# Second attention of a two-layer network: steps that cover one key tile of both heads of a pair

## The chip, the cores and the metric

The kernel runs on one core of one Trainium2 chip. The metric is the device time of one execution in microseconds, median over runs. TensorE is called PE here, VectorE DVE, ScalarE ACT and GpSimd POOL, as in the profile.

## The reference

Six stages follow each other on x of shape (8, 512, 128): expert feed-forward, banded attention, expert feed-forward, then a second kind of feed-forward, a second attention and that feed-forward again. Only the second attention is touched. It has 16 heads of 8 dimensions, for each of 8 chunks of 512 rows:

```python
q_norm_sq = jnp.sum(q * q, axis=-1, keepdims=True)
k_norm_sq = jnp.sum(k * k, axis=-1)[:, :, None, :]
qk = jnp.einsum('bhnd,bhmd->bhnm', q, k)
diff_sq = jnp.maximum(q_norm_sq + k_norm_sq - 2.0 * qk, 0.0)
denom = jnp.maximum((1.0 - CURV * q_norm_sq) * (1.0 - CURV * k_norm_sq), 1e-06)
cosh_arg = jnp.maximum(1.0 + 2.0 * CURV * diff_sq / denom, 1.0)
distance = jnp.where(cosh_arg > 1.0, jnp.arccosh(jnp.maximum(cosh_arg, 1.0 + 1e-12)), 0.0)
attn = jax.nn.softmax(-distance, axis=-1)
out = jnp.einsum('bhnm,bhmd->bhnd', attn, v)
```

With u = diff_sq / denom, the weight is (sqrt(u) + sqrt(1 + u)) to the power -2, which the kernel computes as a root, a root, a sum, a logarithm and an exponential.

## The kernel before

The second attention is the function `attn1`. A chunk has 16 heads, and for each head a matrix of 512 keys (4 key tiles of 128 partitions) by 512 queries. It is worked off in four bursts (b0 to b3) of four heads. A burst has 8 steps; a step covers two key tiles (a half) of one head, so head h = n // 2 and half = n % 2 for step n. The engines run these programs, each in its own order, joined by semaphores:

- PE, `difference(n)` (line 1605): two matmuls with 28 rows of K into two PSUM banks, banks 0 and 1 or 2 and 3 in turn. They read partitions r to r + 28 of KT and QT, where r = 64 * (h % 2). `factor(n)` (line 1617): two matmuls with 9 rows from partition r = 64 * (h % 2) + 32 into banks 4 and 5. The start partition is what sets the row group of the array, so both matmuls of a step use the same one.
- DVE, `relu(n)` (line 1477): U = max(difference, 0), from PSUM into one of four U slots, 1024 elements a partition. `scale(n)` (line 1485): U = min(factor, clamp) * U. The order is relu(n0), then for i = 0 to 7: relu(n0 + i + 1), scale(n0 + i), and then the work that `after0` to `after3` hang on step i: copies of turned rows (line 1321), the OUT copy (line 1383), the division, the norm's copy.
- ACT: for the first two heads of a burst Y = sqrt(U + 1) (line 1443) and U = sqrt(U) (line 1444) head by head, then the same for the last two heads in one (the joined root, 4096 elements a partition), a table load, then the logarithm (line 1449) and the exponential (line 1451) for each pair, and a table load back.
- POOL: Y = Y + U for each head (line 1401), which frees the head's U slot (`t_ready`); between bursts it prepares rows.
- PE, `outputs` (line 1587): the products of weights and values of a pair of heads, for the key tiles named, into bank 7 (OUT). At the end of a pair they free its two Y slots (`pvh_done`). There are six Y slots; the joined root of a burst waits for the products of the pair of three pairs earlier. Even pairs stand inside a burst (`pair_in_burst`), odd ones in the window between bursts, before the first factor of the next burst.
- The window between bursts on PE: `ahead` (two differences of the next burst), then for b0 and b3 `turn_four` (four blocks of transposes, line 1313, copied by DVE), for b1 the projections (line 1206), on whose results DVE works before its first relu, for b2 the output projection (line 458), whose sum and statistics DVE takes before its first relu; then a pair's products.

Inside bursts PE also has transposes hung on single steps: turns at i = 0 to 3 of b0 and b3, the division's in b1 and its turn back at i = 4, the norm's turn (i = 4) and scores (line 1376, i = 5) in b3.

Of the kernel before, what the change touches and what calls it, by code (L numbers as in the profile page):

```python
# [5 lines left out]
ALU = mybir.AluOpType  # L6
# [7 lines left out]
P = 128  # L14
B, S, D = 8, 512, 128
TOK = B * S
TPC = S // P
TILES = TOK // P
H, HD = 16, 8
# [15 lines left out]
def macaron(nc, x, alpha, w_qkv0, bias_rows0, wo0, wo0_t, wfc0, router0, expert_bias, up0, down0,  # L35
            w_qkv1, wo1, router1, up1, down1, out, stop_after=99):
    ctx = ExitStack()
    with ctx:
# [6 lines left out]
        ps = ctx.enter_context(nc.psum_tensor("ps", [P, 8, 512], F32))  # L45
# [1083 lines left out]
        def attn1():  # L1129
            name, lay, nxt = "A1", 1, 1  # L1130
            s = sems[name]
# [3 lines left out]
            UR, YR = 4, 6  # L1135
            SETS = H // 4
            PAIRS = H // 2
            ROWS = 6
            HALVES = 2 * H
            TURNS = 2 * GR  # L1140
            EARLY = TURNS // 2
            VC = 16
            with ExitStack() as st:
# [7 lines left out]
                QT = ab("QT", [P, GR, S], F32R)  # L1151
                KT = ab("KT", [P, GR, S], F32R)
                OT = ab("OT", [P, SETS, S])
                Um = ab("U", [P, UR, TPC, S])
# [37 lines left out]
                    return ps[:, bank, :].rearrange("p (h d) -> p h d", d=HD)  # L1192

                def d_pair(n):
                    return ps[:, 2 * (n % 2):2 * (n % 2) + 2, :].rearrange("p b q -> p (b q)")

                def g_pair():
                    return ps[:, 4:6, :].rearrange("p b q -> p (b q)")

                def u_half(h, half):  # L1200
                    return Um[:, h % UR, 2 * half:2 * half + 2, :].rearrange("p t q -> p (t q)")


                def project_rows_tensor(eng, src, part, bank, done):
# [180 lines left out]
                def body(block):  # L1385
# [46 lines left out]
                    @block.scalar  # L1432
                    def _(eng):
                        def main(c, m, first):
                            for h0 in range(0, H, 4):
                                for h in (h0, h0 + 1, h0 + 2):
                                    joined = h == h0 + 2
                                    y = y_two(m, h) if joined else flat(y_slot(m, h))
                                    u = u_two(h) if joined else flat(Um[:, h % UR])
                                    if not first or h >= YR:  # L1440
                                        eng.wait_ge(s["pvh_done"], c * PAIRS + h // 2 - 1)
                                    eng.wait_ge(s["u_ready"], c * HALVES + 2 * h + (4 if joined else 2))
                                    eng.activation(y, u, ACT.Sqrt, bias=1.0)  # L1443
                                    eng.activation(u, u, ACT.Sqrt).then_inc(s["s_ready"], 2 if joined else 1)  # L1444
                                eng.preload_act_table_set("natural_log_exp_and_others")
                                for h in (h0, h0 + 2):
                                    y = y_two(m, h)
                                    eng.wait_ge(s["t_ready"], c * H + h + 2 + UR)
                                    eng.activation(y, y, ACT.Ln)
                                    eng.drain()  # L1450
                                    eng.activation(y, y, ACT.Exp, scale=-2.0).then_inc(s["y_exp"], 2)  # L1451

                        main(0, 0, True)
                        main(1, 1, False)
                        with eng.Fori(0, (B - 2) // TURN) as k:
                            for i in range(TURN):
                                main(TURN * k + (i + 2), (i + 2) % TURN, False)
                        barrier(eng, b0)

                    @block.vector  # L1460
                    def _(eng):
# [6 lines left out]
                        def main(c, m, first):  # L1468
# [1 line left out]
                            before_c = last_chunk(c)  # L1470

                            def relu(n):
                                h, half = n // 2, n % 2
                                if half == 0:
                                    eng.wait_ge(s["t_ready"], c * H + h + 1)
                                eng.wait_ge(s["d_done"], c * HALVES + n + 1)
                                eng.tensor_scalar(u_half(h, half), d_pair(n), 0.0, None,  # L1477
                                                  ALU.max).then_inc(s["dp_vector"], 1)

                            def scale(n):  # L1480
                                h, half = n // 2, n % 2
                                eng.wait_ge(s["g_done"], c * HALVES + n + 1)
                                eng.wait_ge(s["dp_vector"], c * HALVES + n + 1)
                                u = u_half(h, half)
                                eng.scalar_tensor_tensor(out=u, in0=g_pair(), scalar=CLAMP, in1=u, op0=ALU.min,  # L1485
                                                         op1=ALU.mult).then_inc(s["u_ready"], 1)

# [13 lines left out]
                            def after0(i):  # L1501
                                if i < 4:
                                    turned_vector(eng, c, EARLY + 4 + i)
                                if tail and i == 4:
                                    out_copy_vector(eng, c - 1, 2)
                            burst(0, after0)

# [17 lines left out]
                                add_back_vector(eng, c, before_c)  # L1525

                            def after2(i):
                                if i == 4:
                                    out_copy_vector(eng, c, 0)
                            burst(2, after2)  # L1530

# [4 lines left out]
                            def after3(i):  # L1536
                                if i < 4:
                                    turned_vector(eng, c + 1, 4 + i)
                                if i == 4:
                                    out_copy_vector(eng, c, 1)  # L1540
                                    if tail:
                                        copy_norm_vector(eng, c)
                                if tail and i == 5:
                                    norm_logits_vector(eng, s, c, before_c, nxt, ROWS)
                            burst(3, after3)
# [22 lines left out]
                    def _(eng):  # L1568
# [23 lines left out]
                        def main(c, m, first):  # L1592
                            before_m = (m + TURN - 1) % TURN

                            def difference(n):

                                h, half = n // 2, n % 2
                                if half == 0 and h % 2 == 0:
                                    eng.wait_ge(s["turned"], c * TURNS + h + 2)
                                if not (first and n < 2):  # L1600
                                    eng.wait_ge(s["dp_vector"], c * HALVES + n - 1)
                                r = 64 * (h % 2)
                                for b in range(2):
                                    kt = 2 * half + b
                                    last = eng.matmul(ps[:, 2 * (n % 2) + b, :], KT[r:r + 28, h // 2, kt * P:(kt + 1) * P],  # L1605
                                                      QT[r:r + 28, h // 2, :], start=True, stop=True)
                                last.then_inc(s["d_done"], 1)

                            def factor(n):

                                h, half = n // 2, n % 2
                                if not (first and n == 0):
                                    eng.wait_ge(s["u_ready"], c * HALVES + n)
                                r = 64 * (h % 2) + 32
                                for b in range(2):
                                    kt = 2 * half + b
                                    last = eng.matmul(ps[:, 4 + b, :], KT[r:r + 9, h // 2, kt * P:(kt + 1) * P],  # L1617
                                                      QT[r:r + 9, h // 2, :], start=True, stop=True)
                                last.then_inc(s["g_done"], 1)

                            def burst(g, after):
# [20 lines left out]
                                turn_tensor(eng, k, i0 + 3, WINDOW_BANKS[3])  # L1642

                            def pair_in_burst(n, m, pair, i):
                                if i in (5, 6):
                                    outputs(n, m, pair, (i - 5,))
                                if i == 7:
                                    outputs(n, m, pair, (2, 3))


# [1 line left out]
                            eng.wait_ge(s["turned"], c * TURNS + EARLY)  # L1652
                            if not first:
                                eng.wait_ge(s["lg_copied"], c + 1)
                                eng.wait_ge(s["u_ready"], c * HALVES)
# [17 lines left out]
                            eng.wait_ge(s["u_ready"], c * HALVES + 8)  # L1673
# [31 lines left out]
                            eng.wait_ge(s["u_ready"], c * HALVES + 24)  # L1705
# [111 lines left out]
```

## Time and profile before

| | us |
|---|---|
| median of 3 runs | 3403.89 |
| lowest, highest | 3403.35, 3407.71 |
| profiled execution, its own time | 3406.81 |
| its span in the trace | 3405.1 |
| PE busy | 2960.9 |
| DVE busy | 2218.9 |
| ACT busy | 1886.1 |
| POOL busy | 875.4 |

Busy times are sums over the whole program, of which the second attention is about a third (from 1828 us to some 2960 us). They don't say which engine bounds a stage; waits and timelines do. PE's busy time is made of modelled latencies, so a high share isn't a sign of a full array.

### The profile page before, as it was taken

What the parts mean: (1) busy time and instruction counts of PE and PEld (TensorE: products, weight loads), DVE (VectorE), ACT (ScalarE), POOL (GpSimd) and SP (SyncE); (2) the same over time, 40 slices, a digit from 0 to 9 for tenths busy, and PEclk for the clock granted to TensorE, in tenths of its full rate; (3) what the DMA queues carried; (4) which work ended last, traced back from release to release, by engine and by line L of the source; (5) the groups of instructions that cost most, each with busy time, mean ns of one, the idle gap of its engine ahead of it and who ended that gap; (6) DMA issues with size and microseconds to landing.
All of it is one profiled execution on the core that took longest, in us unless ns stands there. A gap on an engine that the chain in (4) does not pass through costs nothing. (4 is left out here: it accounts for less than half of the span.)

```text
span 3405.1 us, 52318 instructions
## 1 busy us (share of the span) xinstructions
PE 2960.9 (87%) x17860; PEld 2181.0 (64%) x17862; DVE 2218.9 (65%) x5046; ACT 1886.1 (55%) x2052; POOL 875.4 (26%) x584
## 2 busy tenths in 40 slices
PE   5999968888769998799995889898898888489999
PEld 4888846666668887699993333333343333279998
DVE  5555557777645555666666677777777777366665
ACT  2222246767622222343343989989898898533333
POOL 1000010000000000200003566666665667310000
PEclk9999979999979999899996666666666666599999
DMA  2000000000000000000000000000000000100000
GB/s 81 0 0 0 0 1 1 0 0 0 0 0 0 0 0 11 39 0 0 0 0 0 1 0 1 1 0 1 0 1 0 0 0 0 50 1 0 0 0 25
DMA packets 3224, 18.43 MB, mean 5 GB/s; under 512 B 1088, under 2 KB 2112, under 8 KB 2112
## 3 DMA queue, kind: packets, MB, share of 16 engines
q1 hardware_dynamic: 3136, 17.32, 1.3%
q8 instruction: 48, 0.79, 0.1%
q14 instruction: 40, 0.33, 0.0%
HBM read 15.22 MB, written 2.10 MB: 5 GB/s over the span
## 5 line engine op out<-in xcount | busy, mean ns | idle before, releaser
L1401 POOL TENSOR_TENSOR A_Y<-A_Y,A_U 128x2048 f32<-128x2048 f32 x86 | 389.5, 4551 | 260.3 <-ACT A_U L1444 260.3
L1617 PE MATMUL ps<-A_QT,A_KT 9*128 9x512 f32 x512 | 287.1, 655 | 141.8 <-DVE A_U L1485 108.8
L140 POOL TENSOR_TENSOR rstd<-var_eps,half_neg 128x4 f32<-128x4 f32 x45 | 49.8, 1107 | 1208.6 <-DVE var_eps L120 1183.0
L1485 DVE SCALAR_TENSOR_TENSOR A_U<-ps,A_U 128x1024 f32<-128x1024 f32 x256 | 311.4, 1217 | 69.4 <-PE ps L1617 69.4
L1477 DVE TENSOR_SCALAR A_U<-ps 128x1024 f32<-128x1024 f32 x256 | 308.8, 1217 | 59.3 <-PE ps L1605 58.3
L1617 PEld LDWEIGHTS ps<-A_QT,A_KT 9*128 9x128 f32 x512 | 117.1, 283 | 293.2 <-DVE A_U L1485 234.0
L257 ACT ACTIVATE F1b_act<-ps 128x512 f32<-128x512 f32 x256 | 153.3, 599 | 248.0 <-PE ps L223 232.0
L257 ACT ACTIVATE F1a_act<-ps 128x512 f32<-128x512 f32 x256 | 153.2, 599 | 242.8 <-PE ps L223 226.5
L1605 PE MATMUL ps<-A_QT,A_KT 28*128 28x512 f32 x512 | 262.2, 622 | 1.8 <-DVE A_KT L1321 1.6
L257 ACT ACTIVATE F0b_act<-ps 128x512 f32<-128x512 f32 x160 | 95.7, 598 | 272.8 <-PE ps L223 272.8
L257 ACT ACTIVATE F0a_act<-ps 128x512 f32<-128x512 f32 x160 | 95.7, 598 | 265.1 <-PE ps L223 265.1
L231 PEld LDWEIGHTS ps<-dn,F1a_hT 128*128 128x128 f32 x2048 | 237.2, 192 | 4.4
L231 PEld LDWEIGHTS ps<-dn,F1b_hT 128*128 128x128 f32 x2048 | 237.2, 192 | 4.4
L1587 PE MATMUL ps<-A_Y,A_VA 128*32 128x512 f32 x688 | 238.3, 839 | 1.9 <-ACT A_Y L1451 1.9
L231 PE MATMUL ps<-dn,F1a_hT 128*128 128x128 f32 x2048 | 237.6, 275 | 0.0
L231 PE MATMUL ps<-dn,F1b_hT 128*128 128x128 f32 x2048 | 237.6, 275 | 0.0
L1444 ACT ACTIVATE A_U<-A_U 128x2048 f32<-128x2048 f32 (+1 forms) x96 | 236.5, 2463 | 0.0
L1401 POOL TENSOR_TENSOR dn<-dn,A_U 128x2048 f32<-128x2048 f32 x42 | 190.5, 4560 | 134.0 <-ACT A_U L1444 134.0
L841 ACT ACTIVATE A_M<-A_M,A_nmax 128x192 f32<-128x192 f32 (+1 forms) x512 | 203.8, 471 | 34.8 <-DVE A_nmax L956 33.4
L1443 ACT ACTIVATE A_Y<-A_U 128x2048 f32<-128x2048 f32 (+1 forms) x64 | 159.4, 2490 | 83.0 <-DVE A_U L1485 45.1
L1605 PEld LDWEIGHTS ps<-A_QT,A_KT 28*128 28x128 f32 x512 | 116.3, 274 | 137.9 <-issue 120.1
L956 DVE CUSTOM_DVE_ANT_0 A_M<-ps,A_mask 128x192 f32<-128x192 f32 (+1 forms) x512 | 169.3, 387 | 50.1 <-PE ps L1007 49.3
(336 smaller groups left out, 6704.1 us busy)
## 6 DMA issues: line engine op xcount, KB each, us to landing
dn<-in_down SPq DMA_DIRECT2D x2, 2048.0 KB, 12.5
stage<-in_up SPq DMA_DIRECT2D x1, 2560.0 KB, 9.4
X<-in_x SPq DMA_DIRECT2D x1, 2048.0 KB, 7.7
F1a_up<-in_up SPq DMA_DIRECT2D x1, 2048.0 KB, 8.0
F1b_up<-in_up SPq DMA_DIRECT2D x1, 2048.0 KB, 8.0
out_x<-X SPq DMA_DIRECT2D x1, 2048.0 KB, 6.3
dn<-in_down SPq DMA_DIRECT2D x1, 1280.0 KB, 12.0
qkv_w_s<-in_w_qkv SPq DMA_DIRECT2D x2, 192.0 KB
```

The lines of the kernel that those rows point to most:

```text
L231: last = eng.matmul(ps[:, 4 + d % 2, t * P:(t + 1) * P], hT[:, d % 2, hb, t * P:(t + 1) * P], dn[:, d, hb, :], start=(hb == 0), stop=(hb = ...
L257: eng.activation(act_out[:, j % RING, :], ps[:, (j * G) % 4, :], ACT.Silu if lay == 0 else ACT.Relu).then_inc(s["act_done"], 1)
L841: last = eng.activation(m, m, ACT.Exp, scale=-1.0, bias=nmax[:, n % MR, b, r:r + 1])
L956: last = eng.tensor_tensor_reduce(M[:, n % MR, b, r, w0:w1], ps[:, 2 * (n % 2) + b, r * WIN + w0:r * WIN + w1], mask[:, w0:w1], -1.0, 3e38 ...
L1401: eng.tensor_tensor(flat(y_slot(m, h)), flat(y_slot(m, h)), flat(Um[:, h % UR]), ALU.add).then_inc(s["t_ready"], 1)
L1443: eng.activation(y, u, ACT.Sqrt, bias=1.0)
L1444: eng.activation(u, u, ACT.Sqrt).then_inc(s["s_ready"], 2 if joined else 1)
L1477: eng.tensor_scalar(u_half(h, half), d_pair(n), 0.0, None, ALU.max).then_inc(s["dp_vector"], 1)
L1485: eng.scalar_tensor_tensor(out=u, in0=g_pair(), scalar=CLAMP, in1=u, op0=ALU.min, op1=ALU.mult).then_inc(s["u_ready"], 1)
L1587: last = eng.matmul(ps[j:j + 32, OUT, :], VA[:, v0:v0 + 32], y_slot(m, h)[:, kt, :], start=(kt == 0), stop=(kt == TPC - 1))
L1605: last = eng.matmul(ps[:, 2 * (n % 2) + b, :], KT[r:r + 28, h // 2, kt * P:(kt + 1) * P], QT[r:r + 28, h // 2, :], start=True, stop=True)
L1617: last = eng.matmul(ps[:, 4 + b, :], KT[r:r + 9, h // 2, kt * P:(kt + 1) * P], QT[r:r + 9, h // 2, :], start=True, stop=True)
```

## The change

A step covers one key tile of both heads of a pair instead of two key tiles of one head. For step n, pair = n // 4 and the key tile kt = n % 4. The two matmuls of a step now read from partitions 0 and 64 (differences) or 32 and 96 (factors). DVE writes key tile kt of two U slots. Waits follow: DVE's first step of a pair waits until the U slots of both heads are free, ACT's roots wait until the four steps of the pair are scaled. `HALVES` becomes `STEPS`, with the same value. The products of the pair inside a burst move from steps i = 5, 6, 7 to 4, 5, 6 (the first key tile after factor 4, the second after factor 5, the last two after factor 6 and so before factor 7). The OUT copies on DVE move from i = 4 to i = 3.

```diff
-                def u_half(h, half):
-                    return Um[:, h % UR, 2 * half:2 * half + 2, :].rearrange("p t q -> p (t q)")
+                def u_step(n):
+                    h, kt = 2 * (n // TPC), n % TPC
+                    return Um[:, h % UR:h % UR + 2, kt, :]
...
-                                    eng.wait_ge(s["u_ready"], c * HALVES + 2 * h + (4 if joined else 2))
+                                    eng.wait_ge(s["u_ready"], c * STEPS + TPC * (h // 2 + 1))
...
                             def relu(n):
-                                h, half = n // 2, n % 2
-                                if half == 0:
-                                    eng.wait_ge(s["t_ready"], c * H + h + 1)
-                                eng.wait_ge(s["d_done"], c * HALVES + n + 1)
-                                eng.tensor_scalar(u_half(h, half), d_pair(n), 0.0, None,
-                                                  ALU.max).then_inc(s["dp_vector"], 1)
+                                pair, kt = n // TPC, n % TPC
+                                if kt == 0:
+                                    eng.wait_ge(s["t_ready"], c * H + 2 * pair + 2)
+                                eng.wait_ge(s["d_done"], c * STEPS + n + 1)
+                                eng.tensor_scalar(u_step(n), d_pair(n), 0.0, None, ALU.max).then_inc(s["dp_vector"], 1)
...
-                                if tail and i == 4:
+                                if tail and i == 3:
                                     out_copy_vector(eng, c - 1, 2)
...
-                                if i == 4:
+                                if i == 3:
                                     out_copy_vector(eng, c, 0)
...
-                                if i == 4:
+                                if i == 3:
                                     out_copy_vector(eng, c, 1)
-                                    if tail:
-                                        copy_norm_vector(eng, c)
+                                if tail and i == 4:
+                                    copy_norm_vector(eng, c)
...
-                                r = 64 * (h % 2)
                                 for b in range(2):
-                                    kt = 2 * half + b
-                                    last = eng.matmul(ps[:, 2 * (n % 2) + b, :], KT[r:r + 28, h // 2, kt * P:(kt + 1) * P],
-                                                      QT[r:r + 28, h // 2, :], start=True, stop=True)
+                                    r = 64 * b
+                                    last = eng.matmul(ps[:, 2 * (n % 2) + b, :], KT[r:r + 28, pair, kt * P:(kt + 1) * P],
+                                                      QT[r:r + 28, pair, :], start=True, stop=True)
...
-                                r = 64 * (h % 2) + 32
                                 for b in range(2):
-                                    kt = 2 * half + b
-                                    last = eng.matmul(ps[:, 4 + b, :], KT[r:r + 9, h // 2, kt * P:(kt + 1) * P],
-                                                      QT[r:r + 9, h // 2, :], start=True, stop=True)
+                                    r = 64 * b + 32
+                                    last = eng.matmul(ps[:, 4 + b, :], KT[r:r + 9, pair, kt * P:(kt + 1) * P],
+                                                      QT[r:r + 9, pair, :], start=True, stop=True)
...
                             def pair_in_burst(n, m, pair, i):
-                                if i in (5, 6):
-                                    outputs(n, m, pair, (i - 5,))
-                                if i == 7:
+                                if i in (4, 5):
+                                    outputs(n, m, pair, (i - 4,))
+                                if i == 6:
                                     outputs(n, m, pair, (2, 3))
```

## Rows read from the trace of the kernel before

**Rows 1.** The page's 40 slices of the span, TensorE's granted clock in tenths.

```profile
PEclk9999979999979999899996666666666666599999
```

**Rows 2.** Waits from 1828 to 2950 us: us in total, times, longest.

```profile
ACT A_Y L1443 <- PE ps L1587: 37.6, 9, 7.4
...
ACT dn L1443 <- PE ps L1587: 23.4, 4, 7.9
```

**Rows 3.** Timeline of ACT: start us, us, instruction, idle before and its releaser.

```profile
1890.98 3.62 ACT L1443 ACTIVATE A_Y<-A_U 128x4096 f32<-128x4096 f32 x1 [3.43 <-PE ps L1587]
...
2356.34 1.91 ACT L1443 ACTIVATE A_Y<-A_U 128x2048 f32<-128x2048 f32 x1
...
2388.46 1.91 ACT L1443 ACTIVATE dn<-A_U 128x2048 f32<-128x2048 f32 x1
...
2396.52 3.62 ACT L1443 ACTIVATE A_Y<-A_U 128x4096 f32<-128x4096 f32 x1 [0.75 <-PE ps L1587]
...
2436.68 3.62 ACT L1443 ACTIVATE dn<-A_U 128x4096 f32<-128x4096 f32 x1 [7.93 <-PE ps L1587]
...
2849.16 3.62 ACT L1443 ACTIVATE dn<-A_U 128x4096 f32<-128x4096 f32 x1 [5.72 <-PE ps L1587]
```

**Rows 4.** Timeline of POOL, b0 of chunk 4.

```profile
2392.25 9.07 POOL L1401 TENSOR_TENSOR dn<-dn,A_U 128x2048 f32<-128x2048 f32 x2 [9.30 <-ACT A_U L1444]
2403.73 9.05 POOL L1401 TENSOR_TENSOR A_Y<-A_Y,A_U 128x2048 f32<-128x2048 f32 x2 [2.41 <-ACT A_U L1444]
```

**Rows 5.** Timeline of DVE, b0 of chunk 4 up to the start of b1.

```profile
2373.25 0.68 DVE L1321 CAST A_QT<-ps 128x512 fp32r<-128x512 f32 x1
2373.85 1.21 DVE L1477 TENSOR_SCALAR A_U<-ps 128x1024 f32<-128x1024 f32 x1
2374.98 1.21 DVE L1485 SCALAR_TENSOR_TENSOR A_U<-ps,A_U 128x1024 f32<-128x1024 f32 x1
...
2380.84 1.21 DVE L1485 SCALAR_TENSOR_TENSOR A_U<-ps,A_U 128x1024 f32<-128x1024 f32 x1
...
2392.88 1.23 DVE L1485 SCALAR_TENSOR_TENSOR A_U<-ps,A_U 128x1024 f32<-128x1024 f32 x1 [1.31 <-PE ps L1617]
2400.44 1.22 DVE L1230 CAST up_hi<-ps 128x1024 fp32r<-128x1024 f32 x1 [6.34 <-PE ps L1206]
...
2409.87 2.35 DVE L1477 TENSOR_SCALAR A_U<-ps 128x1024 f32<-128x1024 f32 x2
```

**Rows 6.** Timeline of PE, the tail of b0 and the window before b1.

```profile
2386.11 1.92 PE L1587 MATMUL ps<-A_Y,A_VA 128*32 128x512 f32 x4
2387.96 0.79 PE L1605 MATMUL ps<-A_QT,A_KT 28*128 28x512 f32 x1
2387.97 0.79 PE L1617 MATMUL ps<-A_QT,A_KT 9*128 9x512 f32 x1
...
2391.62 1.22 PE L1617 MATMUL ps<-A_QT,A_KT 9*128 9x512 f32 x2 [0.59 <-DVE A_U L1485]
...
2396.33 2.07 PE L1605 MATMUL ps<-A_QT,A_KT 28*128 28x512 f32 x4
2398.33 3.48 PE L1206 MATMUL ps<-qkv_w_s,A_xa 128*128 128x128 f32 x16
...
2402.63 3.63 PE L1587 MATMUL ps<-A_Y,A_VA 128*32 128x512 f32 x16
```

**Rows 7.** Timeline, PE and DVE: pieces of b3, of the window before b0, of that before b2.

```profile
2350.65 1.88 PE L1376 MATMUL ps<-rw,xT_c 128*128 128x8 f32 x8
...
2364.68 1.11 PE L1313 MATMUL ps<-ident,up_hi 128*128 128x128 f32 x4
...
2368.67 2.34 DVE L1477 TENSOR_SCALAR A_U<-ps 128x1024 f32<-128x1024 f32 x2
...
2438.48 2.08 PE L458 MATMUL ps<-out_w,A_oT 128*128 128x128 f32 x8
...
2443.08 2.35 DVE L1477 TENSOR_SCALAR A_U<-ps 128x1024 f32<-128x1024 f32 x2
```

More of the change, by code:

```diff
@@ L1138, in attn1 @@
             ROWS = 6
-            HALVES = 2 * H
+            STEPS = 2 * H
             TURNS = 2 * GR
@@ L1194, in d_pair @@
                 def d_pair(n):
-                    return ps[:, 2 * (n % 2):2 * (n % 2) + 2, :].rearrange("p b q -> p (b q)")
+                    return ps[:, 2 * (n % 2):2 * (n % 2) + 2, :]
                 def g_pair():
-                    return ps[:, 4:6, :].rearrange("p b q -> p (b q)")
-                def u_half(h, half):
-                    return Um[:, h % UR, 2 * half:2 * half + 2, :].rearrange("p t q -> p (t q)")
+                    return ps[:, 4:6, :]
+                def u_step(n):
+                    h, kt = 2 * (n // TPC), n % TPC
+                    return Um[:, h % UR:h % UR + 2, kt, :]
                 def project_rows_tensor(eng, src, part, bank, done):
@@ L1472, in relu @@
                             def relu(n):
-                                h, half = n // 2, n % 2
-                                if half == 0:
-                                    eng.wait_ge(s["t_ready"], c * H + h + 1)
-                                eng.wait_ge(s["d_done"], c * HALVES + n + 1)
-                                eng.tensor_scalar(u_half(h, half), d_pair(n), 0.0, None,
-                                                  ALU.max).then_inc(s["dp_vector"], 1)
+                                pair, kt = n // TPC, n % TPC
[3 more added lines that the diff above has]
+                                eng.tensor_scalar(u_step(n), d_pair(n), 0.0, None, ALU.max).then_inc(s["dp_vector"], 1)
                             def scale(n):
[L1481 to L1484, printed above, removed]
+                                eng.wait_ge(s["g_done"], c * STEPS + n + 1)
+                                eng.wait_ge(s["dp_vector"], c * STEPS + n + 1)
+                                u = u_step(n)
                                 eng.scalar_tensor_tensor(out=u, in0=g_pair(), scalar=CLAMP, in1=u, op0=ALU.min,
@@ L1595, in difference @@
                             def difference(n):
-                                h, half = n // 2, n % 2
-                                if half == 0 and h % 2 == 0:
-                                    eng.wait_ge(s["turned"], c * TURNS + h + 2)
+                                pair, kt = n // TPC, n % TPC
+                                if kt == 0:
+                                    eng.wait_ge(s["turned"], c * TURNS + 2 * pair + 2)
                                 if not (first and n < 2):
-                                    eng.wait_ge(s["dp_vector"], c * HALVES + n - 1)
@@ L1602, in difference @@
-                                r = 64 * (h % 2)
+                                    eng.wait_ge(s["dp_vector"], c * STEPS + n - 1)
                                 for b in range(2):
-                                    kt = 2 * half + b
-                                    last = eng.matmul(ps[:, 2 * (n % 2) + b, :], KT[r:r + 28, h // 2, kt * P:(kt + 1) * P],
-                                                      QT[r:r + 28, h // 2, :], start=True, stop=True)
+                                    r = 64 * b
@@ L1607, in difference @@
+                                    last = eng.matmul(ps[:, 2 * (n % 2) + b, :], KT[r:r + 28, pair, kt * P:(kt + 1) * P],
+                                                      QT[r:r + 28, pair, :], start=True, stop=True)
                                 last.then_inc(s["d_done"], 1)
                             def factor(n):
-                                h, half = n // 2, n % 2
+                                pair, kt = n // TPC, n % TPC
                                 if not (first and n == 0):
-                                    eng.wait_ge(s["u_ready"], c * HALVES + n)
@@ L1614, in factor @@
-                                r = 64 * (h % 2) + 32
+                                    eng.wait_ge(s["u_ready"], c * STEPS + n)
                                 for b in range(2):
-                                    kt = 2 * half + b
-                                    last = eng.matmul(ps[:, 4 + b, :], KT[r:r + 9, h // 2, kt * P:(kt + 1) * P],
-                                                      QT[r:r + 9, h // 2, :], start=True, stop=True)
+                                    r = 64 * b + 32
@@ L1654, in main @@
                                 eng.wait_ge(s["lg_copied"], c + 1)
-                                eng.wait_ge(s["u_ready"], c * HALVES)
+                                eng.wait_ge(s["u_ready"], c * STEPS)
                             turn_four(c, EARLY)
@@ L1672, in main @@
                             project_rows_tensor(eng, xa, 0, 6, "q_done")
-                            eng.wait_ge(s["u_ready"], c * HALVES + 8)
+                            eng.wait_ge(s["u_ready"], c * STEPS + 8)
                             project_rows_tensor(eng, xa, 1, 4, "k_done")
@@ L1704, in main @@
                                 eng.wait_ge(s["x_added"], c)
-                            eng.wait_ge(s["u_ready"], c * HALVES + 24)
+                            eng.wait_ge(s["u_ready"], c * STEPS + 24)
                             turn_four(c + 1, 0)
```

## Prediction

> **What bounds the kernel now.** I read the slices of the span first: the second attention holds the slices where the granted clock sits at 6 tenths [rows 1]. PE looks 87% busy there, but those are latencies at a low clock, so I went to the waits of that stretch. ScalarE (ACT) is the engine with least slack: a burst of four heads costs it 2388.46 - 2356.34 = 32.12 us without a stall [rows 3], 128.5 us for the four bursts b0 to b3 of a chunk. Yet from the first b1 to the last (7 chunks) the joined root moves from 1890.98 to 2849.16, which is 136.9 us a chunk [rows 3]. Nearly all of the 8.4 us between is ACT waiting for a Y slot, that is for weight-value products: 37.6 + 23.4 = 61.0 us in 13 waits [rows 2]. The largest sits in b1 (7.93 us at 2436.68) [rows 3].
>
> Why are the products late? The chain is VectorE (DVE) and PE in turn. In a burst's tail (b0 of chunk 4) a factor pair is issued at 2391.62 and its scale starts at 2392.88 [rows 5, 6]: 1.26 us, two matmuls one behind the other in the same row group. In front of it stand the products, 1.85 us of PE per key tile. After the last scale (ends 2394.1) PE still has two key tiles of products until 2396.33, then two differences (2.0 us), then the projections at 2398.33; DVE gets its next work at 2400.44 and starts b1 at 2409.87 [rows 5, 6]. So DVE and PE, not ACT, set the pace.
>
> **The change, part by part.** Let S be the end of a burst's eighth scale, E that of its fourth, J the start of ACT's joined root.
>
> *Pairing.* The two matmuls of a step go to row groups 0 and 64 (factors 32 and 96) instead of one. The trace has such pairs: at 2387.96 and 2387.97 a difference and a factor of different groups start 0.01 us apart, 0.79 us each, and 4 matmuls take the time of two [rows 6]. I take a pair of one kind as the same: 0.59 us of PE (before 1.15), and 0.83 us from issue to DVE (before 1.26). Bounds: 1.15 (no overlap) and 0.59. The DVE operations now write two rows of 512 with a gap; the strided conversion of 1024 elements at 2400.44 takes 1.22 us like the others [rows 5], so 0; adds and roots keep their shapes, 0. No instruction, DMA or semaphore is added.
>
> *Tail with outputs at i = 4, 5, 6.* DVE steps are 1.13 us apart, a 512 copy 0.60 [rows 5]. Times from E, clock low, b0: copy and OUT copy to 1.12, relu 5 to 2.25, scale 4 to 3.38. PE: factor 4 at 0.05, first product waits for the OUT copy (1.25) and ends 3.10, difference 6 visible 3.93; relu 6, scale 5 end 6.19; second product 4.2 to 6.05, difference 7 visible 6.88; relu 7, scale 6 end 9.14; factor 6, then the two last products 7.1 to 10.65; factor 7 visible 11.48; S = 12.7. The same for b2 (no turned copy): 12.1. For b1 the turn back (1.05, as one turn at 2364.68) stands before difference 6: 13.1. For b3 the norm's turn (1.05) and the scores (1.81, 2350.65) stand inside too [rows 7]: 15.0. Before, b0 took 12.06 (2380.84 + 1.21 to 2392.88 + 1.23) [rows 5], so its tail to S gets longer by 0.6 us: the two last products now delay factor 7. The others gain length by the same mechanism. But before, ACT had to wait on for products until S + 2.3; now they end 2.0 us ahead of S, and PE is free at S - 1.45 instead of S + 2.3.
>
> *Windows between bursts.* Two differences need 1.2 instead of 2.0 us, so PE is through at S - 0.25. b1: projection to DVE 2.1, DVE's row work 9.43 (2400.44 to 2409.87) [rows 5, 6]: first relu at S + 11.3 (before 15.8). b0, b3: turn_four waits for S (its banks are the factors'), then 4.0 us (2364.68 to 2368.67) [rows 7]: S + 4.0. b2: project_out to relu 4.6 (2438.48 to 2443.08) [rows 7]: S + 4.3. Before, all three began 3.7 us later on PE's side (S + 2.3 against S - 1.45) and had the 2.0 us of differences ahead.
>
> *First half of a burst.* Nine DVE steps and up to three copies: 12.0 us (b1 11.9; b2 10.3), plus about 1 where factor 0 stands behind a whole pair's products.
>
> Unhindered, the chain would be b0 4.0 + 13.0 + 12.7 = 29.7, b1 11.3 + 11.9 + 13.1 = 36.3, b2 4.3 + 11 + 12.1 = 27.4, b3 4.0 + 13.0 + 15.0 = 32.0: 125.4, under ACT's 128.5.
>
> *The new waits.* relu of a pair's first step now waits for the adds of both heads that leave its U slots; ACT's first root waits for four steps instead of two. The second costs nothing: E lies well before ACT's next burst. The first does cost. GpSimd's last add ends at 2403.73 + 9.05 = 2412.8, 16.3 us after J = 2396.52 [rows 3, 4]. Before, relu 6 needed that one; now relu 4 does, so E >= J + 16.3 + 2.3 = J + 18.6 of the burst before. Behind relu 4 on DVE stand the scales, the turned copies and the OUT copy, and PE's second half waits for them. Then S >= J + 18.6 + tail, against the next root at J + 32.12:
> - b0: 31.3, no wait, S 0.8 ahead of J.
> - b1: the window decides: -0.8 + 36.3 = 35.5, with 0.15 for the semaphore 35.65; ACT waits 3.5.
> - b2: 30.7, no wait, S 1.4 ahead.
> - b3: 33.6, with the semaphore 33.75; ACT waits 1.6.
>
> A chunk is 32.12 + 35.65 + 32.12 + 33.75 = 133.6 us.
>
> **Sum.** Seven chunks: 7 x (133.6 - 136.9) = -23.1. Chunk 0 (no tail work, wait of 3.43 at 1890.98 [rows 3] goes): -3.4. The last b3, which ran at 32.12, takes 33.75: +1.6. Together -25 us. The profiled execution took 3406.81 us, 2.9 above the runs' median: 3382 on its own terms, 3379 as a median.
>
> **Rivals.**
> - *The matmuls of one kind don't overlap.* Tails grow by about 1.3 (three pairs at 0.43 to 0.56), b1's window by 1: b0 32.6, b1 39.1, b2 32.2, b3 35.1, a chunk 139: +17 us, 3421. It decides from a PE time of about 0.93 us a pair, where the chunk is back at 136.9. The rows speak against it: groups decide, not the kind. 5%.
> - *The windows stay at 1.2 GHz.* The steps use PE less densely, and the full clock in a window arrives only after a run of products: a whole pair takes 3.63 us at 2402.63 but one key tile 1.92 at 2386.11 [rows 6], so about 7.1 cold. Worked out: b0's factor 0 comes at S + 10.6, E at S + 21.2, S at 33.9; b1 38.6 (DVE's value copy waits for the products); b3 34.9: a chunk 139.5, +20 us, 3424. It decides where the pair's products lengthen by about 2 of these 3.5 us in each window. Against it: the products at i = 6 now run just ahead of the windows, as dense as before. 8%. The Trainium skill, TensorE: Matmul & The Clock Gate, Part 1, says that "the default state is throttled, and activity releases the throttle"; by that rule thinner steps could cost full clock, and the time would be this rival's.
> - *ACT's ceiling.* The add coupling and my b1 tail are overstated, ACT never waits: 8 x -8.4 = -67, 3337; everything better than -50 counts here. 7%.
> - *Gains and longer tails cancel*, within 0.2% of 3404: 6%.
>
> **How the numbers follow.** Forecast 3379, 74%. Its own range: b1's and b3's tails are good to about 1.2 us each, so 2.4 a chunk, 20 us: 3357 to 3398. The range 3355 to 3400 leaves out the ceiling's best and both slow rivals, under 2 in 10. Within 0.2% (7 us, about what this kernel's measurement can tell from no change): 0.06. Faster 0.74 + 0.07, rounded with the slow rivals' mild ends 0.82; slower 0.12.
>
> **What would show it.** Difference pairs starting within 0.02 us of each other. ACT's joined root in b1 released by DVE's scale instead of products, waiting 2 to 5 us (7.93 in chunk 4 before). A new wait of DVE's relu (L1477) on GpSimd's add in b0, b2 or b3, and a small ACT wait in b3. DVE idle ahead of b1's window about 2 us instead of 6.3. In the tail, scale 7 waiting about 2.3 us for factor 7. The prediction is wrong if pairs start 0.57 us apart, if the whole pair's products in the windows run at 1.2 GHz, or if ACT still waits for products.

## The result and the profile after

The changed kernel takes 3347.18 us (median of 4 runs, 3345.29 to 3353.39) against 3405.17 for the kernel before beside it; the ratio is 0.9828, interval 0.9813 to 0.9843. That is 58 us less, where 25 were forecast; the time lies below the stated range. A later comparison of the same two kernels on one chip gave 0.984 (0.9826 to 0.9854). The profiled execution took 3349.0 us, its span is 3347.2. In it the second attention's first relu starts 4.6 us earlier than in the trace before (1827.94 against 1832.54), which belongs to the stages ahead of it and not to the change: over all the traces of this document that start lies between 1827.5 and 1836.5 us, though the code ahead of it is the same. From the first relu to the end of the kernel the trace before has 1572.6 us and that of the changed kernel 1519.3, 53.3 us less; a second trace of the changed kernel (changed_again) gives the same 1519.3. So some 53 to 55 us are the change's own.

The waits of the attention from 1828 to 2900 us in the changed kernel (us in total, times, longest):

```profile
DVE A_U L1478 <- POOL A_Y L1402: 64.7, 25, 4.8
...
ACT A_Y L1444 <- DVE A_U L1484: 50.6, 10, 41.4
...
DVE A_U L1478 <- POOL dn L1402: 30.0, 12, 4.9
...
ACT dn L1444 <- DVE A_U L1484: 3.6, 5, 1.5
```

One more row of the same view as [rows 2], of the kernel before:

```profile
ACT A_Y L1443 <- DVE A_U L1485: 45.1, 3, 36.1
```

Two things are to be seen beside [rows 2]. No row of ACT's roots names PE any more: the 61.0 us of waits for products are gone. What the roots still wait for is DVE's scale, 50.6 + 3.6 us, of which 41.4 are the one wait ahead of the first burst. So 12.8 us in 14 waits are left, where the kernel before had 9.0 us in 2 such waits beside its 61.0. (In both kernels ACT's logarithm also waits 0.55 us in each burst for GpSimd's last add, 17 to 18 us in all.) And DVE has a new wait, 94.7 us in 37, on GpSimd's adds, which free the U slots.

The timeline of ACT in the changed kernel, joined roots of b1 in chunks 1, 4 and 7 (beside [rows 3]):

```profile
2011.30 3.62 ACT L1444 ACTIVATE dn<-A_U 128x4096 f32<-128x4096 f32 x1 [0.61 <-DVE A_U L1484]
...
2399.52 3.62 ACT L1444 ACTIVATE dn<-A_U 128x4096 f32<-128x4096 f32 x1 [0.38 <-DVE A_U L1484]
...
2791.99 3.62 ACT L1444 ACTIVATE dn<-A_U 128x4096 f32<-128x4096 f32 x1 [0.47 <-DVE A_U L1484]
```

From 2011.30 to 2791.99 are six chunks: 130.1 us each. Forecast was 133.6, before it was 136.9, and ACT without a stall needs 128.5.

The timeline of PE in the window before b1, in chunk 3 and in chunk 4 (beside [rows 6]):

```profile
2231.49 3.63 PE L1586 MATMUL ps<-A_Y,A_VA 128*32 128x512 f32 x8
2235.05 0.79 PE L1614 MATMUL ps<-A_QT,A_KT 9*128 9x512 f32 x2
2235.06 1.22 PE L1603 MATMUL ps<-A_QT,A_KT 28*128 28x512 f32 x4
2236.21 3.78 PE L1207 MATMUL ps<-qkv_w_s,A_xa 128*128 128x128 f32 x16
...
2360.70 3.24 PE L1586 MATMUL ps<-A_Y,A_VA 128*32 128x512 f32 x8
2363.86 0.50 PE L1614 MATMUL ps<-A_QT,A_KT 9*128 9x512 f32 x2
2363.87 0.74 PE L1603 MATMUL ps<-A_QT,A_KT 28*128 28x512 f32 x4
2364.54 2.31 PE L1207 MATMUL ps<-qkv_w_s,A_xa 128*128 128x128 f32 x16
```

The products now stand ahead of factor 7, and factor 7 and the four differences, in four row groups, start together: 6 matmuls in 1.15 us (2235.06 to 2236.21) at 1.2 GHz. In chunk 4 the granted clock went from 0.50 to 1.00 at 2363.41, just before the last products ended, and the same six take 0.67 us (to 2364.54), the projections 2.31 instead of 3.78.

DVE in those two windows (beside [rows 5]):

```profile
2235.89 1.23 DVE L1484 SCALAR_TENSOR_TENSOR A_U<-ps,A_U 128x1024 f32<-128x1024 f32 x1 [2.27 <-PE ps L1614]
2238.32 1.23 DVE L1231 CAST up_hi<-ps 128x1024 fp32r<-128x1024 f32 x1 [1.21 <-PE ps L1207]
...
2247.74 2.35 DVE L1478 TENSOR_SCALAR A_U<-ps 128x1024 f32<-128x1024 f32 x2
...
2364.41 1.23 DVE L1484 SCALAR_TENSOR_TENSOR A_U<-ps,A_U 128x1024 f32<-128x1024 f32 x1 [1.59 <-PE ps L1614]
2365.73 1.23 DVE L1231 CAST up_hi<-ps 128x1024 fp32r<-128x1024 f32 x1
...
2375.16 2.34 DVE L1478 TENSOR_SCALAR A_U<-ps 128x1024 f32<-128x1024 f32 x2
```

DVE waits 1.21 us for the projections in chunk 3 and not at all in chunk 4, against 6.34 before. From the end of the last scale to b1's first relu are 10.6 and 9.5 us, where the prediction had 11.3 and the kernel before 15.8 in these two chunks.

The granted clock, from 2000 to 2790 us. The figures after the stretch's length are busy times of PE, PEld, DVE, ACT and POOL; the clock is the figure before the DMA share. Of pair_only (see the experiments):

```profile
2000.00:2790.00 790.00, 619.64 (x2242) 244.79 (x2242) 585.90 (x681) 735.67 (x283) 508.00 (x293) 0.63 0.00 1
```

The same of place_only:

```profile
2000.00:2790.00 790.00, 699.76 (x2327) 302.21 (x2328) 615.84 (x712) 761.22 (x291) 533.39 (x314) 0.66 0.00 1
```

The same view of the kernel before, 2010 to 2849:

```profile
2010.00:2849.00 839.00, 742.11 (x2345) 320.31 (x2343) 616.83 (x715) 763.60 (x294) 535.01 (x302) 0.63 0.00 1
```

And of the changed kernel, 2000 to 2792:

```profile
2000.00:2792.00 792.00, 607.26 (x2352) 243.57 (x2352) 621.10 (x714) 764.61 (x295) 530.07 (x301) 0.68 0.00 1
```

PE is shown busy 77% of the stretch instead of 88%, and yet its mean clock went up from 0.63 to 0.68 of full. The Trainium skill (TensorE: Matmul & The Clock Gate, Part 1) has activity release the throttle. The trace agrees in so far as in chunk 4 the clock rose during a run of products. The busy share of the whole stretch did not tell the clock here; it is made of latencies, and these are themselves shorter at the full clock and where pairs overlap.

### The profile page after: what moved, and what is told of

The parts are those of the page before. It is cut to its first block and busy times, and to the rows that moved or that the text cites. A ratio compares the mean times of both kernels' runs of the same rounds, so it can differ in the third digit from the quotient of the medians.

```text
span 3347.2 us, 52294 instructions
## 1 busy us (share of the span) xinstructions
PE 2792.1 (83%) x17860; PEld 2081.7 (62%) x17862; DVE 2227.0 (67%) x5046; ACT 1886.0 (56%) x2052; POOL 875.3 (26%) x584
## 5 line engine op out<-in xcount | busy, mean ns | idle before, releaser
L1614 PE MATMUL ps<-A_QT,A_KT 9*128 9x512 f32 x512 | 182.9, 711 | 195.5 <-DVE A_U L1484 162.6
L1614 PEld LDWEIGHTS ps<-A_QT,A_KT 9*128 9x128 f32 x512 | 66.6, 256 | 333.7 <-DVE A_U L1484 235.8
L1586 PE MATMUL ps<-A_Y,A_VA 128*32 128x512 f32 x688 | 228.7, 798 | 5.8 <-DVE A_OT L1384 3.0
L1603 PE MATMUL ps<-A_QT,A_KT 28*128 28x512 f32 x512 | 168.3, 675 | 37.3 <-DVE A_U L1478 32.9
L282 DVE TENSOR_TENSOR F0b_hT<-F0b_act,ps 128x512 f32<-128x512 f32 x160 | 109.4, 688 | 119.1 <-ACT F0b_act L257 118.0
L1444 ACT ACTIVATE A_Y<-A_U 128x2048 f32<-128x2048 f32 (+1 forms) x64 | 159.3, 2489 | 50.8 <-DVE A_U L1484 50.6
## 6 DMA issues: line engine op xcount, KB each, us to landing
dn<-in_down SPq DMA_DIRECT2D x2, 2048.0 KB, 12.5
```

The costliest lines, as they stand in the source:

```text
L1586: last = eng.matmul(ps[j:j + 32, OUT, :], VA[:, v0:v0 + 32], y_slot(m, h)[:, kt, :], start=(kt == 0), stop=(kt == TPC - 1))
L1603: last = eng.matmul(ps[:, 2 * (n % 2) + b, :], KT[r:r + 28, pair, kt * P:(kt + 1) * P], QT[r:r + 28, pair, :], start=True, stop=True)
L1614: last = eng.matmul(ps[:, 4 + b, :], KT[r:r + 9, pair, kt * P:(kt + 1) * P], QT[r:r + 9, pair, :], start=True, stop=True)
```

## The experiments

All times are medians; ratios are to the kernel before on the same chip, with 95% intervals. "Period" is a third of the distance from the end of b1's eighth scale in chunk 4 to that in chunk 7, read from DVE's timeline. The last column is read from the one trace of each kernel: how much shorter than in the trace before the time from the attention's first relu to the end of the kernel is. It leaves out the stages ahead, whose length varies by up to 9 us between executions.

| kernel | us | ratio | interval | period us | attention's gain in the trace, us |
|---|---|---|---|---|---|
| before | 3405 to 3410 | 1 | | 137.6 | 0 (of 1572.6) |
| changed | 3347.18 | 0.9828 | 0.9813 to 0.9843 | 130.8 | 53.3 |
| pair_only | 3387.82 | 0.9932 | 0.9914 to 0.9949 | 134.6 | 20.1 |
| place_only | 3359.36 | 0.9855 | 0.9839 to 0.9872 | 130.6 | 47.4 |
| same_rows | 3404.71 | 0.9985 | 0.9974 to 0.9995 | 136.5 | 2.6 |
| overlap_only | 3347.11 | 0.9802 | 0.978 to 0.9824 | 128.6 | 60.9 |
| two_late | 3386.85 | 0.9926 | 0.9904 to 0.9948 | 135.5 | 12.0 |
| one_by_one | 3360.62 | 0.9858 | 0.9842 to 0.9875 | 132.3 | 42.9 |
| half_add | 3323.85 | 0.9749 | 0.9732 to 0.9765 | 126.2 | 83.9 |
| overlap_and_place | 3342.94 | 0.9807 | 0.979 to 0.9823 | 128.5 | 63.6 |
| turns_last | 3346.71 | 0.9826 | 0.9811 to 0.9841 | 129.4 | 60.6 |
| changed_again | 3351.81 | 0.984 | 0.9826 to 0.9854 | 130.8 | 53.3 |

**First question: which half of the change made the gain?** Theory A: the place of the products, ahead of factor 7 and so of the window. Theory B: the overlap of the pair's matmuls.

*pair_only*: the changed kernel with

```diff
-                                if i in (4, 5):
-                                    outputs(n, m, pair, (i - 4,))
-                                if i == 6:
+                                if i in (5, 6):
+                                    outputs(n, m, pair, (i - 5,))
+                                if i == 7:
                                     outputs(n, m, pair, (2, 3))
```

and the OUT copies back at i = 4.

> The changed steps (one key tile of both heads), but the products stay at the sixth, seventh and eighth step and the OUT copies at i = 4. Theory A (the place of the products, which brings full clock and an early free PE ahead of the windows, made most of the gain): ACT again waits for products in b1, 3375 to 3390 us. Theory B (the overlap of the pair made most of it): under 3365 us.

Measured 3387.82: A's number. Its waits:

```profile
DVE A_U L1478 <- POOL A_Y L1402: 42.8, 22, 3.9
...
ACT A_Y L1444 <- PE ps L1586: 27.5, 10, 5.5
DVE A_U L1478 <- POOL dn L1402: 26.4, 11, 6.4
ACT dn L1444 <- PE ps L1586: 15.2, 5, 5.1
```

ACT waits for products again, 42.7 us in 15, and DVE for the adds, 69.2 us.

*place_only*: the kernel before with the products and the OUT copies where the change puts them.

```diff
-                                if i in (5, 6):
-                                    outputs(n, m, pair, (i - 5,))
-                                if i == 7:
+                                if i in (4, 5):
+                                    outputs(n, m, pair, (i - 4,))
+                                if i == 6:
                                     outputs(n, m, pair, (2, 3))
```

> The kernel before, with the products at the fifth, sixth and seventh step and the OUT copies at i = 3; steps as before. Theory A: 3360 to 3375 us, tails 1 to 2 us longer but windows after them 3 to 5 us shorter. Theory B: serial pairs behind the products lengthen every tail and eat what the windows give, 3395 to 3410 us.

Measured 3359.36, just under A's range of 3360 to 3375 and far from B's. The tails are longer (b1 in chunks 1 to 7: 14.7 to 15.0 us instead of 12.25) and the windows shorter (before b1 9.7 to 11.1 instead of 13.8 to 15.9), in the expected direction and by somewhat more.

*same_rows*: the changed kernel with both matmuls of a step in one row group.

```diff
-                                    r = 64 * b
+                                    r = 0
...
-                                    r = 64 * b + 32
+                                    r = 32
```

> The changed kernel with both matmuls of a step in one row group (both read the even head's rows, so odd heads get the even head's weights; waits, shapes and counts stay). Theory A: 3355 to 3375 us. Theory B, the rival of the prediction on its own terms: 3400 to 3421 us.

Measured 3404.71. Here A was wrong: without the overlap the changed kernel is worth 0.15%, though the products stand in their new place. Beside place_only (3359.36), which has serial pairs and the new place too, the main thing that is new is the waits for both heads (DVE's for two U slots, ACT's for four steps). They cost some 45 us here.

*overlap_only*: the kernel before with each step's second matmul in the other row group.

```diff
-                                r = 64 * (h % 2)
                                 for b in range(2):
+                                    r = 64 * b
...
-                                r = 64 * (h % 2) + 32
                                 for b in range(2):
+                                    r = 64 * b + 32
```

> The kernel before with the second matmul of each step in the other row group (it reads the other head's rows, so half of each head's matrix comes from its neighbour; waits, shapes, order and counts stay). Shows the overlap without the new waits on GpSimd and without moved products. Theory A: 3375 to 3395 us. Theory B: under 3365 us.

Measured 3347.11, which is B's number. Neither theory holds alone: by itself the overlap gives 62 us by the medians (the interval of its ratio allows 60 to 75), the place 50, both together with the new waits 58. The floor explains it. The period of overlap_only is 128.6 us, ACT's own 128.5. Burst by burst, from one eighth scale's end to the next, in chunk 6:

| | b0 | b1 | b2 | b3 | sum |
|---|---|---|---|---|---|
| before | 35.3 | 38.4 | 29.2 | 33.8 | 136.7 |
| pair_only | 31.6 | 37.5 | 31.3 | 35.0 | 135.4 |
| overlap_only | 30.1 | 37.5 | 28.8 | 32.7 | 129.1 |
| place_only | 30.5 | 36.8 | 30.1 | 32.8 | 130.1 |
| changed | 31.0 | 33.9 | 30.7 | 34.2 | 129.8 |

pair_only and overlap_only have the same b1, 5.4 us over ACT's 32.1. overlap_only makes it up in b0 and b2, where DVE runs ahead of ACT. pair_only can't: its first relu of a pair waits until GpSimd has added both heads. The new wait doesn't lengthen the long burst, it takes away the short ones. It costs 41 us here (62 by the overlap alone, 21 with the waits), about as much as with serial pairs in the new place.

How far the wait reaches can be read burst by burst, as the distance from J, the start of ACT's joined root, to E, the end of DVE's fourth scale of the next burst. In b2 and b3 it is 18.6 to 18.8 us in every chunk of changed, pair_only and same_rows. In place_only, overlap_only and overlap_and_place (below), where DVE waits for one head's slot at a time, DVE gets there sooner where nothing else holds it up: 14.1 to 14.2 us in most b3. The difference, 4.5 us, is one add of GpSimd (4.55 us on average). In b3 of chunk 6, changed first, overlap_and_place below (joined root, fifth relu, fourth scale):

```profile
2694.35 3.60 ACT L1444 ACTIVATE dn<-A_U 128x4096 f32<-128x4096 f32 x1
...
2710.73 1.23 DVE L1478 TENSOR_SCALAR A_U<-ps 128x1024 f32<-128x1024 f32 x1 [0.80 <-POOL dn L1402]
2711.87 1.21 DVE L1484 SCALAR_TENSOR_TENSOR A_U<-ps,A_U 128x1024 f32<-128x1024 f32 x1
...
2692.99 3.60 ACT L1443 ACTIVATE dn<-A_U 128x4096 f32<-128x4096 f32 x1
...
2704.86 1.23 DVE L1477 TENSOR_SCALAR A_U<-ps 128x1024 f32<-128x1024 f32 x1 [0.28 <-POOL dn L1401]
2706.00 1.22 DVE L1485 SCALAR_TENSOR_TENSOR A_U<-ps,A_U 128x1024 f32<-128x1024 f32 x1
```

From joined root to the end of the scale are 18.7 and 14.2 us.

**Second question: what in the place is worth it, and what does the coupling to GpSimd still cost?**

*two_late*: the changed kernel with the last two products after factor 7.

```diff
-                                if i == 6:
+                                if i == 7:
                                     outputs(n, m, pair, (2, 3))
```

> The changed kernel with the last two products after factor 7 again (i = 4, 5, 7); the OUT copies stay at i = 3. Theory A' (what the place is worth is that PE is free for the window before S, and in the full clock): most of the place's worth goes, 3375 to 3390 us, near pair_only. Theory B' (the first two products' earlier step matters): under 3360 us.

Measured 3386.85, as pair_only (3387.82), though its four runs lie far apart (3375.7 to 3398.3). So, within that spread, the worth of the place in the changed kernel lies in the last two products standing ahead of factor 7; the first two and the OUT copies are worth nothing that shows. ACT waits for products again (30.4 + 19.6 us).

*one_by_one*: products at each of four steps.

```diff
-                                if i in (4, 5):
+                                if i in (4, 5, 6, 7):
                                     outputs(n, m, pair, (i - 4,))
-                                if i == 6:
-                                    outputs(n, m, pair, (2, 3))
```

> The changed kernel with one product (two matmuls) at each of i = 4, 5, 6, 7: the tail to S shorter by some 1.8 us, PE free and the Y slots free 2 us later. Expected by the tails' account: b3 stops making ACT wait (0.6 us a chunk), b1 stays as it is: 3340 to 3350 us. If the window's early start is what counts (A'), it loses some 1 us a chunk: 3350 to 3360.

Measured 3360.62, a miss of the first number and 0.6 us above the second's range. The tail of b1 shrank to 11.1 to 11.6 us, but ACT waits for products again, 11.6 + 8.2 us: one product after factor 7 is enough to make the Y slots later than the scale.

*half_add*: GpSimd's sum over two of four key tiles.

```diff
-                            eng.tensor_tensor(flat(y_slot(m, h)), flat(y_slot(m, h)), flat(Um[:, h % UR]),
-                                              ALU.add).then_inc(s["t_ready"], 1)
+                            eng.tensor_tensor(flat(y_slot(m, h)[:, 0:2]), flat(y_slot(m, h)[:, 0:2]),
+                                              flat(Um[:, h % UR, 0:2]), ALU.add).then_inc(s["t_ready"], 1)
```

> The changed kernel with GpSimd's sum Y + U over two of the four key tiles only (the other two tiles' weights are left at sqrt(U + 1)). Coupling theory (relu 4 waits for the last add, so E = J + 18.6): DVE's waits on GpSimd go, and with them ACT's in b3 and b1; the 0.55 us wait of the logarithm goes too (18 us in all): 3310 to 3325 us. If the coupling costs nothing, only the logarithm's wait is won: 3328 to 3335 us.

Measured 3323.85, at the coupling theory's upper edge. A burst of ACT is now 31.45 us from joined root to joined root instead of 32.12, since its wait for the add before the logarithm is gone: 32 x 0.67 = 21 us. Of the rest, the roots' waits for DVE beside the first (12.8 us in the changed kernel) shrank to 4.5 us. In the traces the attention is 30.6 us shorter than in the changed kernel, so some 9 us are the coupling of DVE to GpSimd; by the medians, each against its own kernel before, 6 to 10 us. One thing came out otherwise than expected: DVE's waits on GpSimd did not go (60.2 us in 23). DVE only runs further ahead before it meets them, which ACT doesn't feel.

*overlap_and_place*: place_only with the second matmul in the other row group.

> place_only with the second matmul of each step in the other row group (odd data as in overlap_only): overlap and moved products without the new waits on GpSimd. If ACT's 128.5 us a chunk is the floor, it gives no more than overlap_only: 3338 to 3348 us. If place and overlap add up (62 and 50 us), far less: under 3310 us.

Measured 3342.94, period 128.5: ACT's floor. The two don't add up (67 us together, 62 and 50 alone), because either is enough to bring the chain of DVE and PE close to it. The changed kernel has both and the new waits besides. Against their own kernels before it gains 58 us (changed) and 55 (changed_again) where this one gains 67, and in the traces 53.3 where this one gains 63.6. So the new waits still cost some 10 us in the changed kernel, in agreement with half_add. DVE's waits on GpSimd are 69.5 us in 53 here, though after chunk 0 no joined root of ACT waits: how long DVE waits is no measure of what its waits cost.

With that, the waits' price is known in three settings, from medians against the kernel before beside them:

| | without the waits | with them | price |
|---|---|---|---|
| overlap, old place | 62 (overlap_only) | 21 (pair_only) | 41 |
| serial, new place | 50 (place_only) | 4 (same_rows) | 45 |
| overlap, new place | 67 (overlap_and_place) | 55 to 58 (changed) | 9 to 12 |

It takes both the overlap and the place to make the waits cheap. The waits alone, with neither, were not run.

*turns_last* and *changed_again*: the scores of b3 with their addition, and the turn back of b1 with its copy, at i = 7.

```diff
-                                if tail and i == 4:
+                                if tail and i == 7:
                                     copy_back_vector(eng, c)
...
-                                if not first and i == 5:
+                                if not first and i == 7:
                                     score_tensor(eng, c)
```

(and in the same way `turn_back_tensor` and `norm_logits_vector`).

> The changed kernel with the norm's scores and their addition (b3) and the turn back and its copy (b1) at i = 7 instead of i = 5 and i = 4. By the tails' account b3's tail loses the 1.8 us of the scores and b1's the 1.05 us of the turn, so the 0.5 us and 0.5 to 1.5 us by which ACT still waits there go: 7 to 9 us under the changed kernel beside it, about 3338 to 3342 us. If what remains is POOL's coupling and not those tails: no difference.

> The changed kernel once more, for comparison on the same chip: 3343 to 3353 us.

Measured 3346.71 and 3351.81, 5 us apart, ratios 0.9826 and 0.984 with intervals that overlap: the sign is as expected, the size short of the 7 to 9 us, and not beyond the noise. Much of that noise lies ahead of the attention: from the first relu on, the two traces are 7.3 us apart (60.6 and 53.3 us under the one before), in the expected range, though each is one execution. The mechanism shows in the waits of turns_last:

```profile
ACT A_Y L1444 <- DVE A_U L1484: 45.2, 5, 41.5
...
ACT dn L1444 <- DVE A_U L1484: 1.9, 1, 1.9
```

5.6 us of ACT's waits are left beside the first, instead of 12.8. There is little more to win here without a shorter ACT.

## Why the prediction was wrong

The sign and the waits were right. The step that failed is the two terms of the sum in which ACT still waits: b1 with 35.65 us and b3 with 33.75, from joined root to joined root. Over chunks 1 to 7 they measured 33.1 (32.6 to 34.3) and 32.5 (32.1 to 32.9). That is 3.8 us a chunk, 26 us in seven chunks, as much again as the whole forecast: 130.1 us a chunk instead of 133.6. Both came out too long because DVE's tails and b1's window were too long in the sum; in part that was a matmul time, in part the clock, which the prediction had left low.

- *The overlap of a pair*: right. The changed kernel's pairs start within 0.01 us, take 0.79 us from start to end and DVE follows after 0.84 (difference at 2716.76, relu at 2717.60; forecast 0.83). A pair by itself holds PE for 0.73 us (2713.14 to 2713.87 below), not 0.59. The rival of serial pairs was priced at 3421, 17 us over the kernel before, and measured at 3404.71 in same_rows, 4 us under the one beside it. So the overlap does decide, but even the sign of that price was wrong.
- *The waits for products*: right, gone from ACT. *The new wait on GpSimd*: right, down to its formula. In chunk 6 the joined root of b2 starts at 2694.35 and E of b3 is at 2713.08: J + 18.7, predicted J + 18.6.
- *b1's window, "first relu at S + 11.3"*: the part of b1's term that failed most. It measured 9.5 us where its first part, up to the projections, ran at 2.4 GHz (chunks 4, 6, 7), 10.6 where that ran at 1.2 (chunks 1, 3), and 10.0 in chunks 2 and 5. Even at the low clock the six matmuls of factor 7 and the differences took 1.15 us together, which I had counted one behind the other; the full clock, which I had left out of the window, took the rest, and DVE then has no wait for the projections at all.
- *b1's tail of 13.1*: it follows the granted clock. 13.26 us in chunk 2, where the tail's mean clock was 0.50, 12.5 in chunks 4 to 7 at 0.70 to 0.71, 10.95 in chunks 1 and 3 at 0.78. So 13.1 was good for the low clock, at which every b1 tail of the kernel before ran. *b3's tail of 15.0*: 14.0 to 14.1 in chunks 4 to 7 at 0.56 to 0.57, and 11.1 to 12.5 in chunks 0 to 3, at up to 0.80. The PE timeline of b3 in chunk 6 shows the term that was too long even at the low clock: the difference and the factor after each of the first two products start together and take one pair's time.

```profile
2713.14 0.79 PE L1614 MATMUL ps<-A_QT,A_KT 9*128 9x512 f32 x2 [1.19 <-DVE A_U L1484]
2713.87 1.11 PE L1339 MATMUL ps<-ident,xn 128*128 128x128 f32 x4
2714.91 1.92 PE L1586 MATMUL ps<-A_Y,A_VA 128*32 128x512 f32 x4
2716.76 0.79 PE L1603 MATMUL ps<-A_QT,A_KT 28*128 28x512 f32 x2
2716.77 0.79 PE L1614 MATMUL ps<-A_QT,A_KT 9*128 9x512 f32 x2
```

  Four matmuls from 2716.76 to the scores at 2717.49: 0.73 us. I had counted two pairs of 0.59, 1.18, twice in a tail: 0.9 of the 1.0 us by which this tail is shorter than 15.0.
- *The joint effect*: from 2629.50 (joined root of b0 in chunk 6) to 2662.26 are 32.76, and b3 there took 32.80 (2694.35 to 2727.15). Terms of 1 to 2 us each, near a floor of 32.12, doubled the gain. The 0.15 us for the semaphore in both terms stands in no row; where ACT waits for the scale, its root starts 0.03 to 0.04 us after the scale's end.
- *"The windows stay at 1.2 GHz"*: the wrong sign. The windows saw the full clock more, not less: the one before b0 had a mean granted clock of 1.00 in six of seven chunks and 0.61 in the other, against 0.50 to 0.84 in the kernel before. One instruction group is a poor witness for it: of the seven output projections ahead of b2, six took 1.16 us in the changed kernel and the rest 2.08, but five did in the kernel before, four in pair_only and only two in place_only.
- *The ceiling*, at 7%, was what happened, by the bound that the prediction gave it ("everything better than -50 counts here"). Its picture, ACT never waiting, was not quite met: 12.8 us of the roots' waits are left, and its number was 3337. It is overlap_and_place, without the new waits, that comes to ACT's period.

What stays open: how much of the gain is the clock by itself, and what raised it. From 1840 to 2840 us the mean granted clock was 0.62 in the kernel before, 0.64 in pair_only and overlap_only, 0.65 in place_only, same_rows and two_late, 0.67 in the changed kernel and 0.68 in overlap_and_place. So the clock alone doesn't make the time: overlap_only gains 62 us at 0.64, same_rows 4 us at 0.65. But no run changed the clock by itself.

## What to carry to other kernels

Where one engine sets a floor and a chain of others runs just above it, what counts is not the mean of the chain but whether its short bursts can make up for the long one: a wait that ties the producer to the consumer's release of buffers can cost most of what an overlap or a better order gives (41 and 45 us here with one of them, about 10 with both). Before two edits are made together, price each against the floor by itself: here, without the waits, the place alone was worth 50 us and the overlap 62, but the place added only 5 to the overlap. Order the last matmuls of a stage by what waits for them: in the changed kernel two products that free a buffer were worth 32 to 35 us ahead of the last short matmul instead of behind it. And to tell differences of 5 to 10 us in one stage of a long kernel, compare the stage in the traces: here the stages ahead of it varied by up to 9 us.

## What the runs showed of the hardware

- Six matmuls of 512 columns in four row groups (9 and 28 rows each) took 1.15 us at 1.2 GHz and 0.67 us at 2.4 GHz, up to the start of the next instruction. At 1.2 GHz four in four row groups took 0.73 us, as much as two in two (0.73); four in two row groups of the kernel before took 1.16 (2387.96 to 2389.12) and two in one 1.15 (2391.62 to 2392.77).
- The mean granted clock rose from 0.63 to 0.68 while PE's shown busy share fell from 88% to 77%: the shown share did not tell the clock.
- GpSimd's add of 128x2048 took 4.55 us, and DVE's fourth scale came 4.5 us later where it had to wait for one add more.
- A DVE operation of 1024 elements that writes two rows of 512 with a gap takes 1.21 to 1.23 us, the same as one that writes them in one piece.
